# Feed-forward by integer codes: fewer products on TensorE, the scales applied behind PSUM

## The reference

```
w[k, n] = (q[k, n] - (z[g, n] + 1)) * s[g, n],   g = k // 128
y = x + down(silu(x @ gate) * (x @ up))          # 512 -> 1376 -> 512, then the norm
```

## Time and the profile before

| | |
|---|---|
| median of 3 runs | 928.52 us (928.19 to 930.88) |
| the profiled execution | 927.76 us |
| its span, first to last instruction | 926.0 us |
| mean granted TensorE clock | 0.988 |

### The profile page before, as it was taken

The page is one execution under the profiler, slowest core; times in us unless marked ns, Lnnn a source line. Parts: engine busy times, 40 slices in busy tenths (PEclk is TensorE's granted clock), DMA queues, the critical chain, the costliest instruction groups (busy, mean ns, idle before and its releaser), DMA issues.

```text
span 926.0 us, 17345 instructions
## 1 busy us (share of the span) xinstructions
PE 878.3 (95%) x6285; PEld 487.1 (53%) x6285; DVE 701.3 (76%) x1076; ACT 474.1 (51%) x1448; POOL 491.3 (53%) x430
## 2 busy tenths in 40 slices
PE   8888999889799999999999999999998899999997
PEld 3665777555445555555555555545544444444443
DVE  5688887887677888698797887997997545885333
ACT  4777878552555554565565565545655512333000
POOL 1264349526556676578567666768887411331011
PEclk9999999989999999999999999999999999999999
DMA  6754243320135412315234142134333120420001
GB/s 177 230 182 152 70 127 116 103 99 17 24 85 132 104 35 70 103 35 148 35 74 109 32 129 58 24 80 92 72 95 86 35 63 2 141 63 1 12 35 45
DMA packets 119173, 76.22 MB, mean 82 GB/s; under 512 B 72653, under 2 KB 103344, under 8 KB 119088
## 3 DMA queue, kind: packets, MB, share of 16 engines
q1 hardware_dynamic: 116784, 74.45, 30.6%
q10 hardware_dynamic: 2304, 0.66, 0.3%
HBM read 51.96 MB, written 6.36 MB: 63 GB/s over the span
## 4 chain that ended last, share of the span: by engine, by line
PE 58%; DVE 13%; POOL 9%; ACT 8%; issue 8%; DMA 4%; SPq 0%; ACTq 0%; DVEq 0%; POOLq 0%
PE bank L311 17%; PE bank L312 17%; PE bank L313 17%; POOL rot L569 3%; ACT prob L692 2%; DVE nmax L940 2%; POOL pn L586 2%; DVE rsin L1019 2%; POOL q2l L575 1%; DMA pT<-pn 1%; DVE pT L909 1%; ACT prob L834 1%; POOL deq L593 1%; ACT pT L643 1%; PE bank L1442 1%
## 5 line engine op out<-in xcount | busy, mean ns | idle before, releaser
L579 POOL TENSOR_TENSOR prob<-prob,rden 128x512 f32<-128x512 f32 x64 | 66.5, 1039 | 128.7 <-DVE rden L1084 128.6
L569 POOL TENSOR_TENSOR rot<-rcos,rsin 128x512 f32<-128x512 f32 x80 | 106.4, 1331 | 32.3 <-DVE rsin L1019 32.2
L311 PE MATMUL bank<-aTh,xqh 128*128 128x512 f16 x256 | 98.7, 386 | 5.0 <-DVE aTl L909 3.1
L312 PE MATMUL bank<-aTl,xqh 128*128 128x512 f16 x256 | 98.8, 386 | 0.0
L313 PE MATMUL bank<-aTh,xql 128*128 128x512 f16 x256 | 98.5, 385 | 0.0
L311 PE MATMUL bank<-xoh,o2h 128*128 128x512 f16 x256 | 98.3, 384 | 0.1
L312 PE MATMUL bank<-xol,o2h 128*128 128x512 f16 x256 | 98.2, 384 | 0.0
L313 PE MATMUL bank<-xoh,o2l 128*128 128x512 f16 x256 | 97.9, 383 | 0.0
L834 ACT ACTIVATE prob<-bank,ebias 128x128 f32<-128x128 f32 x256 | 90.4, 365 | 2.1
L1019 DVE SCALAR_TENSOR_TENSOR rsin<-bank,sinq 64x512 f32<-64x512 f32 x128 | 88.1, 688 | 1.7
L643 ACT ACTIVATE ebias<-nmax 128x4 f32<-128x4 f32 x128 | 26.9, 210 | 116.3 <-DVE nmax L1079 75.5
(11 more groups left out here) (181 smaller groups left out, 2528.3 us busy)
## 6 DMA issues: line engine op xcount, KB each, us to landing
tst<-tables SPq DMA_DIRECT2D x11, 768.0 KB, 6.2
xqs<-in_xwq SPq DMA_DIRECT2D x8, 1024.0 KB, 6.3
xos<-in_xwo SPq DMA_DIRECT2D x8, 1024.0 KB, 5.5
qst<-in_fq SPq DMA_DIRECT2D x11, 384.0 KB, 3.6
kstk<-stack SPq DMA_DIRECT2D x48, 64.0 KB, 2.3
qstk<-stack SPq DMA_DIRECT2D x21, 128.0 KB, 2.6
xs<-in_ctxT SPq DMA_DIRECT2D x2, 1024.0 KB, 8.1
res<-in_x SPq DMA_DIRECT2D x1, 2048.0 KB, 8.2
```

The costliest lines, as they stand in the source:

```text
L311: pe.matmul(out_ap, ah, bh, start=first, stop=False)
L312: pe.matmul(out_ap, ah, bl, start=False, stop=False)
L569: nc.gpsimd.tensor_tensor(rot[:, r % 2, :], rcos[:, r % 2, :], rsin[:, r % 2, :], ALU.add).then_inc(rope_rot, 1)
L579: nc.gpsimd.tensor_tensor(prob[:, v % 2, :].rearrange("p (h k) -> p h k", h=QH), prob[:, v % 2, :].rearrange("p (h k) -> p h k", h=QH), rd ...
```

## The change

In 14 of the 22 tiles (i from 4 on, `CODED`) TensorE multiplies the integer differences q - z - 1 themselves. They are exact in f16, so a K tile needs two products (codes by aTh and by aTl) and not three. Since each K tile has its own scale, each goes to its own bank: `coded_gate_up` fills eight banks, four of gate and four of up, with two products each (16 for 24). A scale is one number per output row, here a column of 128 partitions (`scol`, from a new small input fc).

- ScalarE takes banks k = 0 and 1 of gate and of up out with a Copy whose scale is that column (`leave_bank`, tile left).
- GpSimd adds the two (`add_left`).
- VectorE adds banks k = 2 and 3, scaled (`add_bank`, tile total), first for gate, and in the next turn of its loop (`finish`) for up.
- silu and gate_times_up then read `total` and not PSUM.

`inter_lo` moves from VectorE to GpSimd for all tiles. The tiles of half 1 of i = 0 to 3, still with three products and now in banks 4 and 5, are spread between the coded ones: after coded tiles 0, 4, 8 and 12. Weights of gate and up from i = 4 on are no longer scaled or split; `dif` is a weight tile itself.

In down, K tiles 7 to 10 (`DOWN_CODES`) are coded too: `down_codes(b)` makes two products each into a bank of their own (6 banks rotate, `part_bank`), VectorE multiplies them by the scales (`scale_part`, tile wds, broadcast by four new DMAs of 128 KB), GpSimd adds the four (`add_parts`), and VectorE adds the sum when it takes the batch out. Products of batch b + 1's codes stand inside down(b), before its fourth K tile; down(b) uses banks 6 and 7 alone.

The diff, cut to what the text speaks of:

```diff
+NSPLIT = 4
+CODED = [(i, h) for i in range(NSPLIT, NI) for h in range(NHALF)]
+GATE_UP = [(i, 0) for i in range(NSPLIT)]
+for c, tile in enumerate(CODED):
+    GATE_UP += [tile] + ([(c // 4, 1)] if c % 4 == 0 else [])
+CODE_BANK = 0, 1, 6, 7, 4, 5, 2, 3
+SPLIT_BANK = 4, 5
+DOWN_CODES = (7, 8, 9, 10)
...
+            def add_left(n, m):
+                pool.wait_ge(f_left, 4 * coded_before(n) + 2 * m + 2)
+                nc.gpsimd.tensor_tensor(left[m][:, 0, :], left[m][:, 0, :], left[m][:, 1, :], ALU.add).then_inc(f_sum, 1)
...
+            for n in range(len(GU_USE), len(GATE_UP)):
+                i, half = GATE_UP[n]
+                if is_coded(n):
+                    add_left(n, 0)
+                    add_left(n, 1)
+                if n > len(GU_USE):
+                    inter_lo(n - 1)
+                if is_coded(n) and half == 0 and i + 1 < DOWN_CODES[0]:
+                    scale_codes(i + 1)
+            inter_lo(len(GATE_UP) - 1)
...
+            def leave_bank(n, m, k):
+                i, c = GATE_UP[n][0], coded_before(n)
+                act.wait_ge(f_cb, 8 * c + 4 * m + k + 1)
...
+                if c >= 1 and k == 0:
+                    act.wait_ge(f_total[m], 2 * c - 1)
+                nc.scalar.activation(left[m][:, k, :], bank[CODE_BANK[4 * m + k]][:, :], ACT.Copy,
+                                     scale=scol[:, i - NSPLIT, m, k:k + 1]).then_inc(f_left, 1)
...
             for n in range(len(GU_USE), len(GATE_UP)):
-                if n % 2 == 0 and n // 2 + 1 < NI and n >= 6:
-                    weights_hi(n // 2 + 1)
+                i, half = GATE_UP[n]
+                if is_coded(n):
+                    for m in range(2):
+                        for k in range(2):
+                            leave_bank(n, m, k)
+                if n > len(GU_USE):
+                    inter_hi(n - 1)
+                if is_coded(n) and half == 0 and i in DOWN_SPLIT:
+                    weights_hi(i)
                 gate_silu(n)
-                inter_hi(n)
+            inter_hi(len(GATE_UP) - 1)
...
+            def add_bank(n, m, k):
...
+                nc.vector.scalar_tensor_tensor(out=total[m][:, :], in0=bank[CODE_BANK[banks]][:, :],
+                                               scalar=scol[:, i - NSPLIT, m, k:k + 1],
+                                               in1=(left[m][:, 0, :] if k == 2 else total[m][:, :]),
+                                               op0=ALU.mult, op1=ALU.add).then_inc(f_total[m], 1)
...
+            def finish(n):
+                if is_coded(n):
+                    add_bank(n, 1, 2)
+                    add_bank(n, 1, 3)
+                gate_times_up(n)
+
             for n in range(len(GU_USE), len(GATE_UP)):
...
+                if n > len(GU_USE):
+                    finish(n - 1)
+                if is_coded(n):
+                    add_bank(n, 0, 2)
+                    add_bank(n, 0, 3)
+                    if half == 0 and i + 1 < NI:
+                        codes(i + 1)
+                    if half == 1 and i in DOWN_SPLIT:
+                        weights_lo(i)
+            finish(len(GATE_UP) - 1)
...
             def add_ffn(b):
                 dve.wait_ge(f_y, b + 1)
-                nc.vector.tensor_scalar(yh[:, b % 2, :], bank[4 + b % 4][:, :], 2.0 ** (-E_I - E_W), None,
-                                        ALU.mult).then_inc(f_y16, 1)
+                dve.wait_ge(f_parts, b + 1)
+                nc.vector.scalar_tensor_tensor(out=yh[:, b % 2, :], in0=bank[6 + b % 2][:, :], scalar=2.0 ** (-E_I - E_W),
+                                               in1=part[:, b % 2, 0, :], op0=ALU.mult, op1=ALU.add).then_inc(f_y16, 1)
...
             for b in range(NB):
                 add_ffn(b)
                 statistics(2, b)
+                if b + 2 < NB:
+                    for e in range(len(DOWN_CODES)):
+                        scale_part(b + 2, e)
                 normalised(2, b)
...
+            def bank_free(n, p):
+                c, m, k = coded_before(n), p // 4, p % 4
+                if c == 0:
+                    first_free(p)
+                elif k >= 2:
+                    pe.wait_ge(f_total[m], 2 * c - 3 + k)
+                elif m == 1 and not is_coded(n - 1):
+                    pe.wait_ge((f_gated, f_inter)[k], n)
+                else:
+                    pe.wait_ge(f_left, 4 * c - 3 + 2 * m + k)
+
+            def coded_gate_up(n):
...
+                for p in range(8):
+                    bank_free(n, p)
+                    dst, w, k = bank[CODE_BANK[p]][:, :], dif[:, i % 2, p * P:(p + 1) * P], p % 4
+                    pe_.matmul(dst, w, aTh[:, k, cols], start=True, stop=False)
+                    pe_.matmul(dst, w, aTl[:, k, cols], start=False, stop=True).then_inc(f_cb, 1)
...
             def down(b):
...
+                for k in DOWN_SPLIT:
+                    if k == DOWN_SPLIT[3] and b + 1 < NB:
+                        down_codes(b + 1)
```

More of the change, by code:

```diff
@@ L266, in decoder_kernel @@
         gated = at(83.5, "gated", [P, 2, HALF], F32)
+        left = [at(kb, f"left{m}", [P, 2, HALF], F32) for m, kb in enumerate((79.5, 8))]
+        total = [at(kb, f"total{m}", [P, HALF], F32) for m, kb in enumerate((12, 14))]
         yh = at(4, "yh", [P, 2, D], F16)
@@ L332, in turn_bank, with part_bank, split_before @@
             return bank[4 + 3 * (u % 2)]
+        def part_bank(use):
+            return bank[(0, 1, 4, 5, 2, 3)[use % 6]]
+        def split_before(i):
+            return sum(1 for k in DOWN_SPLIT if k < i)
         def by_k(tile):
@@ L1123, in codes @@
                 dve.wait_ge(f_nib, i + 1)
-                if i >= 2:
+                if 2 <= i < DOWN_CODES[0] + 2:
                     dve.wait_ge(f_deq, i - 1)
-                nc.vector.tensor_tensor(dif[:, i % 2, :], nib[:, :], tst[:, i % 2, 0, :], ALU.subtract).then_inc(f_dif, 1)
-            def weights_lo(i):
[L1129 to L1132, removed]
-                nc.vector.tensor_tensor(wdl[i][:, :], deq[:, i % 2, 2 * D:], wdh[i][:, :], ALU.subtract).then_inc(f_dlo, 1)
@@ L1490, in down @@
             def down(b):
-                pe.wait_ge(f_ilo, GU_POS[(NI - 1, b // BH)] + 1)
                 if b == 0:
[L1493 to L1499, removed]
+                    pe.wait_ge(f_dlo, len(DOWN_SPLIT))
@@ new lines, in down @@
+                if b < 2:
+                    pe.wait_ge(f_total[0], 2 * len(CODED))
+                else:
+                    pe.wait_ge(f_y16, b - 1)
+                for k in DOWN_SPLIT:
+                    if k == DOWN_SPLIT[3] and b + 1 < NB:
+                        down_codes(b + 1)
+                    last = split_products(pe_, bank[6 + b % 2][:, :], inh[k][:, b * S:(b + 1) * S], inl[k][:, b * S:(b + 1) * S],
+                                          wdh[k][:, :], wdl[k][:, :], k == DOWN_SPLIT[0], k == DOWN_SPLIT[-1])
```

199 lines of the change are left out of this document (156 added, 43 removed).

## The result

The changed kernel takes 914.91 us by the median of 4 runs (913.44 to 917.39), the kernel before beside it 928.36 (927.87 to 930.88): a ratio of 0.9852 [0.9824, 0.9881], 13.5 us less. The forecast was 922.0, 6.2 us less, with a range of 909 to 933. The direction and the range held; the gain is more than twice the forecast one.

The account below looks back on a forecast made before the run. TensorE was taken to bound gate/up and down before the change. Gate/up ends 0.3 plus down 6.9 less clock 1.0 gave 6.2 us saved: median 928.5 to 922, range 909 to 933.

Parts of the forecast that it names:

- Nothing: Side changes, such as the column table, broadcasts and inl of tile 0, cost nothing; 0.6 us if tile 0's cover were gone.
- GpSimd's scaling shrinks: Listed among the work taken away: GpSimd scales fewer weight columns; no place or size given.
- GpSimd's add goes in between: Gate/up cycle with codes(): GpSimd's add runs before VectorE's second difference, to 4.09, delaying that difference to 4.5 us.
- Codes cycles: Gate/up cycles in which VectorE also runs codes(): 7.35 us, or 7.2 where GpSimd scales a down part.
- Clock: Half clock behind most of five TensorE waits of about 3.1 us in gate/up, costing 1.0 us in all.
- Ring: Gate/up loop: silu, next banks, GpSimd's add and gate sums follow each other; 4.76 us, 5.0 with the add begun late.
- wdl: Gate/up cycle where VectorE also makes wdl (i of 4 to 6): 5.35 us.
- split: Gate/up cycle with a split tile between coded ones: 9.9 us; the first 8.9, the last 7.5.
- Fewer collisions: Rival, chance 0.20: nib, dif and gate_times_up find GpSimd between instructions; gate/up cycles take 79 us for 89, total 912.
- More collisions: Rival, chance 0.20: gate_times_up waits for GpSimd's whole add each gate/up cycle, 1.27 for 0.24; 13 us more, 935.
- TensorE as bound: Rival, chance 0.03: TensorE stays the bound in gate/up too; 31.1 + 1.5 us saved, 896.
- The clock: Rival, chance 0.10: TensorE's clock falls in the 5.0 us gate/up cycles too; 933 with eight falls.

Follow-up runs that it names:

- e5: Changed kernel with GpSimd scaling all 1,536 columns for i = 4 again, as in the kernel before; 918.96 us, ratio 0.9903.
- e6: Kernel before, with only the scaling of i = 4 moved three slots later, behind the turns of probabilities; 922.95 us, ratio 0.9952.
- e4: Changed kernel plus a short unused VectorE reduction before the second difference of K tiles 7 to 10; 917.56 us, ratio 0.9885.
- e2: Changed kernel with ScalarE taking the next coded tile's two gate banks out before this tile's silu; 915.45 us, ratio 0.9863.
- e3: e2 plus, around split tiles, both silus first and their inter_hi after the next two gate banks; 913.03 us, ratio 0.9834.
- e7: e3 with the second (down) difference of K tiles 7 to 10 moved behind wdl of the next tile; 915.70 us, ratio 0.9858.

## Why the prediction was right in direction and gave half the gain

Two steps failed, worth 3.6 and 4.0 us.

**The first is the part "Nothing".** It said of the changes ahead of tile 4 that they cost nothing, and asked only for losses. "GpSimd's scaling shrinks" stood under what the change takes away, with no place and no price. Its place was in front of the last-but-one p_lo, and TensorE's wait behind it was the longest in that part. It was worth 3.6 us: 1.88 of waiting and 1.69 of clock (shown by e5 and, in the kernel before, by e6). The chain of waits of the kernel before listed dif, this deq, p_lo and the DMA one after another; the argument began at 769 and never looked there. inl of tile 0 was placed right: no product between the marks waited for the last turn in the changed kernel, so its cover held.

**The second is the walk of the codes cycles, "GpSimd's add goes in between".** It put the add ahead of the second difference and so the up sums 0.8 us too late.
- Codes cycles: 7.35 forecast, 5.96 and 5.86 measured; 7.2 forecast, 6.74 measured. With the differences of the other ten (none over 0.31) the loop took 86.1 us for 89.2: 3.0 us mis-sized. What a collision costs was right (e4); which side of it the kernel is on was decided by 0.3 us that the walk had from estimates.
- Clock: 1.0 us forecast to be lost, none was. The idle time that I set at 3.1 us a cycle was 1.3 to 1.4, because the up sums came earlier.

**The other terms.**
- Ring 5.0 (measured 5.07), wdl 5.35 (5.29), split 9.9 (9.83 and 9.74), first 8.9 (9.21), last 7.5 (7.67): right. So were a bank sum's 0.75, 0.69 for Copy with a column and GpSimd's 1.27, all from nearest rows. The step from a gate sum to the one that waits for it was 0.85 and not 0.78, as much as the ring came out longer.
- First down product 0.75 ahead of the last gate sum: 859.48 - 858.72 = 0.76. Down: 908.84 - 858.72 + 0.22 = 50.3 us for 50.1. Tail the same.
- "Seven wgl differences (4.11 us each)": six took that long, the last 1.22; no term of the sum rests on it.

6.2 + 3.0 + 1.0 + 3.6, less 0.3 in small terms (down 0.2, the start of the loop 0.1), is 13.5 us.

**Rivals.** Fewer collisions (912, 0.20) was nearest in time, and partly by luck, since 3.6 us of the gain came from a place that it doesn't speak of; in kind it is half right: nib takes 1.13 to 1.23 us for 0.61 in five of six codes cycles, still held by GpSimd, and only the second difference gets through. More collisions asked that gate_times_up wait for the whole add in each cycle; it took 0.69 in ten of the fourteen coded tiles and 0.95 to 1.46 in four, so this didn't set the cycle (e2 and e4 made collisions of another kind, of the differences). TensorE as bound is ruled out by its 74 us in 90. The clock did not fall in the loop: its banks rotate with a wait of up to 1.4 us in each cycle, and it stayed at 1.00. The Trainium skill ("TensorE: Matmul & The Clock Gate", "A second HAM failure mode: psum-queue depth-cycling") says that a kernel which cycles PSUM banks and idles briefly between groups of products can oscillate between the two clocks; by that the loop might have lost its gain. The changed kernel's trace doesn't show it, with waits of up to 1.4 us; e2 and e4 show single falls behind waits of 2.56 and 2.69, which is not yet an oscillation.

## What to carry to other kernels

When an edit makes an instruction shorter, find every place where it runs and price each by the wait that stands behind it there, ahead of the region of the edit too; begin with the chain of waits over the whole span. A saving on an engine is worth what the ring that replaces it leaves: 31 us of products fewer gave 10, and the 24 us of them that lie in gate/up gave, by themselves, a loss of 2. Where two engines exclude each other, a walk in tenths of a microsecond decides which goes first, so give both outcomes their own price instead of choosing one.

## What was unexpected of the hardware

- nib, held up by GpSimd, ended 0.42 us after inl's end (842.67 for 842.25), though by itself it takes 0.61; wdc in e4 ended 0.29 after left (816.46 for 816.17) for 0.42 by itself. In both, the blocked instruction of VectorE cost less than the rest of the other's time and its own; starts and ends on GpSimd are rough, so a part of it may be the record. The Trainium skill ("SBUF — State Buffer", section on the two separate sides) calls the shared pair of ports an exclusive lock in which the other fully blocks. Read as a wait of the whole instruction, that would put the ends 0.61 and 0.42 apart. These traces agree that the two hold each other up, but by less than that.
- The same wait of TensorE was followed by half clock once and not another time: 2.34 us ahead of 814.05 in e3 (0.53 from 814.9 to 818.1), and 2.34 ahead of 839.33 in the same run (1.00 throughout). 2.04 us at the first mark left the clock at 1.00 in the changed kernel; 2.01 us ahead of 816.20 in e7 was followed by half clock. What decides it is open; the changed kernel's loop, with no wait over 1.4 us, never showed it.
